# Local attention in 32-query blocks with a reordered chunk, in a program of two local-attention stacks

## What is computed

```python
x = x + attn_a(layernorm(x))
x = x + stack(layernorm(x))      # the diff touches both stacks
x = x + attn_b(layernorm(x))
x = x + stack(layernorm(x))
# stack: 6 times
x = attn_layer(shift_tokens(x)) + x
x = ffn_layer(shift_tokens(x)) + x
# attn_layer: q, k, v of 16 heads x 64; q and k to unit length, scaled, rotary tables;
# window w = 32: block i of 32 queries sees key blocks i - 1 and i (64 keys),
mask = (it < jb) | (it > jb + w) | (jb == -1)      # at most 33 of the 64
attn = softmax(where(mask, -max, q @ k.T * 8)); out = (attn @ v) @ Wo
```

## Time and profile before

| | |
|---|---|
| median of 3 runs | 5310.7 us |
| span of the profiled execution | 5297.4 us |
| PE busy | 4675.9 us, 88% |
| VectorE busy | 4003.6 us, 76% |
| ScalarE busy | 3636.0 us, 69% |
| GpSimd busy | 2657.4 us, 50% |
| queue q1 of DMAs | 331028 packets, 281.93 MB, 20.6% of 16 engines |

### The profile page before, as it was taken

One profiled execution on the slowest core, in us unless ns is written; L12 is line 12 of the kernel. 1 busy time (PEld: TensorE's weight loads), 2 busy tenths in 40 slices (PEclk: granted clock), 3 DMA queues, 4 the chain that ended last, 5 costly groups with the idle time before them and its releaser, 6 DMA issues. The chain is left out here.

```text
span 5297.4 us, 148317 instructions
## 1 busy us (share of the span) xinstructions
PE 4675.9 (88%) x45796; PEld 2897.7 (55%) x45796; DVE 4003.6 (76%) x8097; ACT 3636.0 (69%) x11780; POOL 2657.4 (50%) x2108
## 2 busy tenths in 40 slices
PE   5999999698898998989989767989989989899897
PEld 1333332366565665656656544665656656566565
DVE  7888886587786877868778546878868778687785
ACT  1777777586785876858768514867858778587684
POOL 3000000465665666656656404656656566566564
PEclk6999999899999999999999977999999999999998
DMA  0000000222222222222222302222222222222223
GB/s 13 1 2 1 2 1 1 85 59 72 59 59 77 59 71 60 59 77 59 64 66 60 83 7 85 59 73 59 57 78 59 72 62 57 77 60 69 65 56 93
DMA packets 332305, 288.20 MB, mean 54 GB/s; under 512 B 149102, under 2 KB 290964, under 8 KB 329748
## 3 DMA queue, kind: packets, MB, share of 16 engines
q1 hardware_dynamic: 331028, 281.93, 20.6%
q10 hardware_dynamic: 768, 0.02, 0.0%
HBM read 100.42 MB, written 30.41 MB: 25 GB/s over the span
## 5 line engine op out<-in xcount | busy, mean ns | idle before, releaser
L929 POOL TENSOR_TENSOR g_rn<-g_ss,g_minus_half 128x8 f32<-128x8 f32 x384 | 636.8, 1658 | 299.7 <-DVE g_ss L1077 297.0
L929 POOL TENSOR_TENSOR f_rn<-f_ss,f_minus_half 128x8 f32<-128x8 f32 x384 | 636.8, 1658 | 299.2 <-DVE f_ss L1077 295.9
L425 DVE TENSOR_REDUCE a_maxima<-a_max 128x1 f32<-128x512 f32 x1024 | 651.3, 685 | 148.4 <-PE a_max L539 142.2
L1003 ACT ACTIVATE f_ex<-f_bank,f_nmx 128x96 f32<-128x96 f32 x1536 | 501.5, 338 | 226.8 <-DVE f_nmx L1082 226.8
L1003 ACT ACTIVATE g_ex<-g_bank,g_nmx 128x96 f32<-128x96 f32 x1536 | 501.6, 338 | 226.6 <-DVE g_nmx L1082 226.6
L349 ACT ACTIVATE a_pex<-a_scores 128x512 f32<-128x512 f32 x1024 | 531.7, 607 | 159.6 <-PE a_scores L548 159.6
L934 POOL TENSOR_TENSOR f_qr<-f_t 128x512 f32<-128x512 f32 x384 | 488.4, 1272 | 268.8 <-DVE f_t L1100 268.8
L934 POOL TENSOR_TENSOR g_qr<-g_t 128x512 f32<-128x512 f32 x384 | 488.2, 1271 | 269.0 <-DVE g_t L1100 269.0
L1172 PE MATMUL g_bank<-g_wqkv,g_xT 128*128 128x512 f32 x768 | 407.2, 613 | 30.4 <-ACT g_xT L977 24.3
L1172 PE MATMUL f_bank<-f_wqkv,f_xT 128*128 128x512 f32 x768 | 406.4, 612 | 29.2 <-ACT f_xT L977 24.5
L1077 DVE TENSOR_REDUCE g_ss<-g_sq 128x8 f32<-128x512 f32 x384 | 263.1, 685 | 207.9 <-ACT g_sq L985 207.9
(11 more groups left out here) (244 smaller groups left out, 11909.8 us busy)
## 6 DMA issues: line engine op xcount, KB each, us to landing
f_vw<-f_vt SPq DMA_DIRECT2D x96, 384.0 KB, 4.3
g_vw<-g_vt SPq DMA_DIRECT2D x96, 384.0 KB, 4.3
f_vw<-f_vt SPq DMA_DIRECT2D x96, 256.0 KB, 3.5
g_vw<-g_vt SPq DMA_DIRECT2D x96, 256.0 KB, 3.5
f_vw<-f_vt SPq DMA_DIRECT2D x96, 128.0 KB, 2.3
g_vw<-g_vt SPq DMA_DIRECT2D x96, 128.0 KB, 2.3
f_wqkv<-in_f_Wqkv_dram SPq DMA_DIRECT2D x7, 1536.0 KB, 9.5
g_wqkv<-in_f_Wqkv_dram SPq DMA_DIRECT2D x7, 1536.0 KB, 9.3
```

The source lines that it names most:

```text
L425: dve.tensor_reduce(maxima[:, m // 4, m % 4:m % 4 + 1], ps_max[m % 3][:], AX.X, ALU.max).then_inc(dv_max, 1)
L929: pool.tensor_tensor(rn[:, b, :], ss[:, b, :], minus_half[:], ALU.pow).then_inc(pl_rn, 1)
L1003: last = act.activation(ex[:, b, u, :], ps_s[:, h, KEYS * jj:KEYS * jj + KEYS], ACT.Exp, bias=nmx[:, b, u:u + 1], accum_out=sm[:, b, u:u + 1])
```

## The change

- `BLK` goes from 64 to 32 (`NB` = 4 blocks per tile), so a block has 64 keys (`KEYS`) instead of 96.
- Scores: 16 products per chunk with 32 queries as weights and 64 keys moving, on eighths of the array (64x32). `kT` holds the keys of two tiles side by side, 128 columns each; an even tile's first block takes its previous keys from the other end of the buffer, in another order than the rest, and the mask has a form for it. The copy of the keys' tail and its semaphore go.
- Masks: 4 matmuls (64x64 parts) instead of 2.
- Probabilities: two tiles of 64 keys are turned together: 2 turnings of 128 columns instead of 4 of 96, and one copy of 128x256 instead of 96x512.
- Values: 16 products with 64 rows, on quarters of the array. `vw` holds 4 blocks, for two groups of heads in the two halves of the partitions: 10 DMAs per tile instead of 3. `vt`'s columns are ordered by pair for it. `ps_pT` and `ps_o` share a pair of banks, so the values wait for the copy of the probabilities turned in the same chunk.
- Output projection in halves, at c = 2 and c = 3; the values' projection at c = 0 and 1; the residual's addition at the end of c = 3 for tile t - 2 instead of t - 3 a chunk later.
- Order of the chunk on PE: projection, turning of q/k (n - 3 instead of n - 2), turning of probabilities, values' projection or half an output projection, values, masks and scores, x. On ScalarE: xT, exponentials (n - 5 instead of n - 4), q/k copy, copy of probabilities, squares, values' copy, output copy. On VectorE: rotary products (n - 2 instead of n - 1), normalisation, scaling, maxima, sum of squares, residual.

```diff
-BLK = 64
+BLK = 32
+NB = P // BLK
-        kT = sb("kT", [P, PAIRS, WINDOW + P])
+        kT = sb("kT", [P, PAIRS, 2 * P])
-        vw = sb("vw", [P, 2, 2, INNER])
+        vw = sb("vw", [P, 2, NB, PAIRS // 2 * P])
...
-                    sp.dma_start(vw[0:32, p, 0, :], vt[96:128, 1 - p, :]).then_inc(ld_vw[p], 16)
-                    sp.dma_start(vw[32:96, p, 0, :], vt[0:64, p, :]).then_inc(ld_vw[p], 16)
-                    sp.dma_start(vw[0:96, p, 1, :], vt[32:128, p, :]).then_inc(ld_vw[p], 16)
+                    for jj in range(2):
+                        k, cols = KEYS * jj, slice(512 * jj, 512 * jj + 512)
+                        last, mine = (k, k + WINDOW) if p else (k + BLK, k)
+                        sp.dma_start(vw[last:last + WINDOW, p, 0, :], vt[P - WINDOW:P, 1 - p, cols]).then_inc(ld_vw[p], 16)
+                        sp.dma_start(vw[mine:mine + BLK, p, 0, :], vt[0:BLK, p, cols]).then_inc(ld_vw[p], 16)
+                        for blk in range(1, NB):
+                            r = BLK * blk - WINDOW
+                            sp.dma_start(vw[k:k + KEYS, p, blk, :], vt[r:r + KEYS, p, cols]).then_inc(ld_vw[p], 16)
...
+                    if real(t, c, 3):
+                        pe.wait_ge(pl_qr, upto(pl_qr, L, n - 3))
+                        pe.wait_ge(act_qk, upto(act_qk, L, n - 4))
+                        for j in range(4):
+                            last = pe.transpose(ps_qkT[:, P * j:P * j + P], qr[:, 1 - b, P * j:P * j + P], ident[:])
+                        last.then_inc(pe_qkT, 1)
                     if real(t, c, 6):
...
                         pe.wait_ge(dv_pn, upto(dv_pn, L, n - 6))
+                        pe.wait_ge(act_aT, upto(act_aT, L, n - 8))
                         pe.wait_ge(act_pT, upto(act_pT, L, n - 7))
-                        for u in range(4):
-                            last = pe.transpose(ps_pT[0:KEYS, P * u:P * u + P], pn[:, b, u, :], ident[:])
+                        for h in range(2):
+                            last = pe.transpose(ps_pT[:, P * h:P * h + P],
+                                                pn[:, b, 2 * h:2 * h + 2, :].rearrange("p u c -> p (u c)"), ident[:])
                         last.then_inc(pe_pT, 1)
...
+                        for j in range(4 * half, 4 * half + 4):
+                            last = pe.matmul(ps_y[:, 0:P], aT[:, q, j, :], wo[:, j, :], start=(j == 0), stop=(j == PAIRS - 1))
...
+                        turned = min(n - 6, STEPS - 1) if known else n - 6
+                        pe.wait_ge(act_pT, upto(act_pT, L, turned)).then_inc(own["pe"], 1)
+                        for blk in range(NB):
+                            qs = slice(BLK * blk, BLK * blk + BLK)
+                            for jj in range(2):
+                                k = slice(KEYS * jj, KEYS * jj + KEYS)
+                                for h in range(2):
+                                    r = slice(DH * h, DH * h + DH)
+                                    at = P * g + DH * h
+                                    last = pe.matmul(ps_o[r, jj, qs], vw[k, p, blk, at:at + DH], pT[k, 1 - b, h, qs],
+                                                     start=True, stop=True, tile_position=(KEYS * jj, DH * h))
+                        last.then_inc(pe_o, 1)
...
+                        for jj in range(2):
+                            j = 2 * g + jj
+                            for blk in range(NB):
+                                o = slice(BLK * blk, BLK * blk + BLK)
+                                k0 = (0 if even else P) + BLK * blk - WINDOW
...
+                                    last = pe.matmul(ps_s[o, h, KEYS * jj:KEYS * jj + KEYS].rearrange("p (a k) -> p a k", k=WINDOW),
+                                                     qT[r, j, o], keys, start=False, stop=(jj == 1), tile_position=(DH * h, BLK * blk))
+                        last.then_inc(pe_s, 1)
```

More of the change, by code:

```diff
@@ L61, in host_tables @@
     seen = (c[None, :] >= q[:, None]) & (c[None, :] <= q[:, None] + WINDOW)
-    rest = np.where(seen, f(0), f(MASKED))
-    first = np.where(seen & (c[None, :] >= WINDOW), f(0), f(MASKED))
-    start = np.where(np.arange(P)[:, None] < BLK, first, rest)
-    mask = np.stack([np.stack([m, m], 1) for m in (start, rest)], 1)
+    odd = np.where(seen, f(0), f(MASKED))
+    before = np.arange(P)[:, None] % DH < BLK
+    even = np.where(before, np.roll(odd, -WINDOW, axis=1), odd)
+    first = np.where(before & (c[None, :] >= KEYS - WINDOW), f(MASKED), even)
+    mask = np.stack([np.stack([m, m], 1) for m in (first, even, odd)], 1)
     theta = (f(1.0) / np.power(f(10000.0), np.arange(0, AD, 2, dtype=f) / f(AD))).astype(f)
@@ L650, in bank @@
             return ctx.enter_context(nc.psum_tensor(f"{tag}_bank{i}", [P, n, 512], F32))
-        one = [bank(i) for i in range(6)]
+        one = [bank(i) for i in range(4)]
+        ps_po = bank(4, 2)
         ps_s = bank(6, 2)
-        banks = [t[:, 0, :] for t in one] + [ps_s[:, 0, :], ps_s[:, 1, :]]
+        banks = [t[:, 0, :] for t in one] + [ps_po[:, 0, :], ps_po[:, 1, :], ps_s[:, 0, :], ps_s[:, 1, :]]
         ps_qk = banks[0:2]
@@ L1147, in _ @@
                 dve.wait_ge(pl_rope, upto(pl_rope, L, 5)).then_inc(own["dve"], 1)
[L1148 removed]
+                layer(dve, tile, group, L, NT + 2)
                 dve.wait_ge(pe_s, upto(pe_s, L, STEPS - 1))
[L1151 removed]
+                dve.memset(kT[:, :, 2 * P - WINDOW:2 * P], 0.0).then_inc(dv_kzero, 1)
         @block.tensor
@@ new lines, in tile @@
+                        last.then_inc(pe_o, 1)
+                    if real(t, c, 4):
+                        g, even = c, q == 1
+                        first = known and t == 1
+                        if first and c == 0:
+                            pe.wait_ge(act_const, 3)
+                        pe.wait_ge(act_qk, upto(act_qk, L, 4 * t - (3 if g < 2 else 1)))
+                        pe.wait_ge(act_exp, upto(act_exp, L, n - 5)).then_inc(own["pe"], 1)
+                        for h in range(2):
+                            r = slice(DH * h, DH * h + DH)
+                            for o in (slice(0, DH), slice(DH, P)):
+                                seen = 2 if o.start or not even else 0 if first else 1
+                                pe.matmul(ps_s[o, h, 0:2 * KEYS], twice_bf[r, o], mask_bf[r, seen, :], start=True, stop=False,
+                                          tile_position=(DH * h, o.start))
@@ L1233, in tile @@
-                        last.then_inc(pe_o, 1)
-                    if c == 3 and real(t - 2, 0, 0):
-                        pe.wait_ge(act_aT, upto(act_aT, L, 4 * t - 5))
-                        pe.wait_ge(act_v, upto(act_v, L, min(2 * t, 2 * NT - 2) + 1 if known else 2 * t + 1))
-                        pe.wait_ge(dv_y, upto(dv_y, L, t - 3))
-                        for j in range(PAIRS):
-                            last = pe.matmul(ps_y[:, 0:P], aT[:, q, j, :], wo[:, j, :], start=(j == 0), stop=(j == PAIRS - 1))
-                        last.then_inc(pe_Wo, 1)
```

216 lines of the change are left out of this document (94 added, 122 removed).

## The result

The changed kernel takes 5255.1 us (median of 4 runs, 5248.4 to 5269.7), the kernel before 5307.6 beside it: ratio 0.991, 95% interval 0.989 to 0.992. It is faster, by 52 us where 336 were forecast, and outside the range of 4830 to 5240. The profiled execution spans 5251.2 (before 5297.4).

The account below looks back on a forecast made before the run. TensorE (PE) was taken as the bound: 14.73 us of work plus waits of 0.2, 0.2 and 0.1 made a tile of 15.25 instead of 17.27. At 28 us per layer, 336 for 12, 5310.7 became 4975 us (range 4830 to 5240).

Parts of the forecast that it names:

- the forecast sum 14.73: PE work per middle tile in us, added up group by group after the change; 1.65 less than before.
- rival (1): Small score and value products on PE don't run eight and four at once: tile 18.8, kernel 5555 us; chance 0.12 in full.
- Rival (2): PE's longer loop body no longer fits the instruction store: 3.5 us per branch, 168 in all, 5143 us; chance 0.12.
- Rival (4): Fewer waits than taken: 14.73 for all 15 intervals, 38.7 us less per layer, kernel 4847 us; chance 0.08.
- All stay below 14.73, so PE remains the bound: Middle tile: VectorE falls to 13.6 and ScalarE to 12.5, so PE's work still sets the tile.
- the new wait: Values on PE wait for the same chunk's copy of turned probabilities: 0 to 0.3 per chunk, taken as 0.05.
- 0.2 per tile, 0 to 1.1: ScalarE's copy of new values waits for the last of ten window DMAs; 0.2 us per tile taken.
- Rival (3): Value windows come late, plus the late copy of probabilities: tile 16.3 to 17, kernel 5080 to 5200 us; chance 0.12.
- Ramps at both ends gain less ... 1.7: Layer ends: 13 of 15 intervals gain in full, plus 1.7 us for the ramps, 28 us per layer.

Follow-up runs that it names:

- comb1: Changed kernel with scores issued ahead of values on TensorE, plus the edits of tail_first and exp_early: 5101.4 us, ratio 0.962 to the kernel before.
- pn_last: ss_first with VectorE's reciprocal and normalization moved behind the maxima: 5271.4 us, ratio 0.992 to the kernel before.
- both: pn_last with scores also issued ahead of values on TensorE; window DMAs as in the changed kernel: 5274.2 us, ratio 0.993 to the kernel before.
- tail_first: Changed kernel with the two window DMAs reading the previous tile's last rows issued first; ScalarE's copy waits for only these of the newest ten: 5174.6 us, ratio 0.975.
- comb2: both with the edits of tail_first and exp_early added: 5076.5 us, ratio 0.956 to the kernel before.
- half_vw: Changed kernel with five of each tile's ten window DMAs left out, so it computes something else: 5167.5 us, ratio 0.975 to the kernel before.
- exp_early: Changed kernel with the exponentials of a layer's last chunk issued at the end of tile 16, ahead of the feed-forward's first group: 5249.2 us, ratio 0.989.
- comb4: comb3 with fewer added identity transposes in tile 17 (3 per place, none ahead of the output projection): 5051.8 us, ratio 0.953 to the kernel before.
- ss_first: Changed kernel with VectorE's sum of squares issued ahead of the maxima in each chunk: 5514.0 us, ratio 1.039 to the kernel before.
- comb3: comb2 with unread identity transposes added on TensorE in each layer's drain: 5094.7 us, ratio 0.959 to the kernel before.

## Why the prediction was wrong, point by point

**TensorE's work: near, 0.1 to 0.3 low.** PE's busy time in a middle tile is 14.86 and 15.27, the forecast sum 14.73, and comb1's tile without idle time has 15.06 from start to start. In the timeline above, 32 values start 0.46 ahead of the masks, the masks 0.20 ahead of the scores, and the next projection starts 0.59 behind the scores (1131.86 to 1132.45). So rival (1) is out: the small products do run side by side, at 226 and 225 ns each but 32 within 0.67 and 0.46. Rival (2) is out too, by the branch of the tile loop (shortest/median/longest ns):

```profile
L762 PEldq COMPARE_BRANCH  x60: 76/212/242, 1071.7 to 5097.3; - x60
```

212 ns, not 3.5 us, for the longer body. VectorE at 13.87 (forecast 13.6) and ScalarE at 12.71 (12.5) are near. Rival (4)'s 38.7 us per layer can't be worked out from its words: 15 intervals of 14.73 against the 249.97 of before, 3 taken off for the ends, is 26, and added 32. Nothing else hangs on it.

**"All stay below 14.73, so PE remains the bound": the step that failed.** It compared sums of busy time and never followed a ring through the engines. The forecast even named the new wait ("they wait for the copy of this chunk ... since both halves lie in one bank ... the 36 instructions of mask and scores queue behind, and VectorE's maximum behind those"), and priced it by the cover ahead of it, at 0.05 per chunk. But the exponentials and the copies ahead of that copy on ScalarE start from the very maxima that queue behind. Its length could have been added up beforehand: scores, mask and values 1.1 and maxima 0.42 by the sum's own steps, the copy of probabilities 0.39, the copy of queries or keys 0.6 and four exponentials 1.3 by the trace of before, less 0.25 where ScalarE's work overlaps, and 0.3 for handing over: near 3.9, against 3.68 of PE work per chunk. (The last two terms were put in with the result known.) Four turns of the measured 3.88 are 15.5, 0.3 of the missing 0.6 of a tile; the other 0.3 is the fourth chunk's, where the maxima come 4.0 or 4.2 to 4.4 apart: no run takes that apart, and a longer fourth chunk is in comb2 too (4.1 to 4.5). The ring is a property of "values ahead of scores" and of one bank for both halves: with the scores first the wait fell from 90.6 to 14.4 (pn_last to both), and with the DMAs' wait gone too every second tile of the loop fell to 15.25 (tail_first to comb1).

**GpSimd was not priced at all.** Its rn grew from 1658 to 1897 ns since the new order puts the normalization onto the end of rn, and the second ring took the maxima in. Neither costs anything as long as the first ring is as long; pn_last shows that. Together with the scores first it matters: 25 us from comb1 to comb2.

**Window DMAs: right mechanism, wrong size.** "0.2 per tile, 0 to 1.1" would be 38 us for 192 tiles. Measured: nothing in the middle tiles, 0.4 to 1.6 in each of six tiles per layer at the ends (half_vw), 80 us in all (tail_first), and the middle tiles too once the rings are gone (both). What the sum lacked is that at the ends an issue is at times twice or three times 0.59; that these long issues make the wait is read from where they stand, no run takes them away. Rival (3), 5080 to 5200 by the DMAs and the late copy together, is the nearest to what happened, though 5255 is above it and the two causes hid each other instead of adding up.

**"Ramps at both ends gain less ... 1.7": wrong.** They gained less than nothing. Besides the DMAs, the drain grew: the result of a layer's last tile comes 32.0 behind that of the tile two before, where it was 26.2. Two causes have a measured size: the exponentials of chunk 63, issued a chunk later than before, fell behind the feed-forward's first copy (1.2 of the last interval, exp_early, though by itself that gave the kernel nothing clear of noise), and TensorE's clock fell to 1.2 GHz with the products at 1.08 instead of 0.67 and half an output projection at 2.07 instead of 1.06 (25 us in all at the least, comb2 to comb4; before, the same stretch ran at 1.00). The trace shows what TensorE did around the fall: it stood idle between the chunks of the drain, where the chain through the other engines sets the pace, 1.24 ahead of the values at 1252.16, 3.66 ahead of the feed-forward's transposes at 1270.09. The drain of the changed kernel also holds a normalization of 1.69 under GpSimd's product for the rotary tables, which wasn't tried by itself.

**What is left.** From 5255 to the 4975 of the forecast are 280 us. The runs account for 80 (DMAs' wait), 98 (rings, held normalization and exponentials, tail_first to comb2) and 25 (clock), to 5052. These shares go by the order of the edits: since the limits hide each other, another order would share them out otherwise. Of the last 77, some 24 are the loop's tiles (15.33 and 15.62 instead of 15.25, 9 by 0.22 by 12); most of the rest lies in the drain (the last two intervals take 27.6 where the forecast had some 24) and wasn't taken apart.

## What to carry to other kernels

When one engine is the fullest by busy time, add up every ring that an order by hand closes (each engine's queue order counts as an edge, and so does each wait for a shared bank) and compare the longest with the fullest engine's work per turn; a wait "covered" by work that itself depends on what queues behind the wait is not covered. When an experiment that removes a likely cause changes nothing, don't strike the cause: remove it together with its neighbours, since limits of a tuned kernel stand close together. And let a buffer's writer wait for those reads alone that touch what it overwrites: two DMAs of ten, here 80 us.

## What the runs showed of the hardware

**VectorE and GpSimd hold each other up.** A normalization that starts while GpSimd's addition runs (both read their inputs from SBUF) ends 0.28 behind the addition's end, at 1.44 instead of 0.42. In the changed kernel and comb1 one that starts 1.04 to 1.5 us into rn takes its 0.42, and rn 1.81 to 2.12 instead of 1.65; in pn_last, both and comb2 one that starts 0.2 to 1.0 into rn changes neither. With the normalization behind the maxima the means are 424 and 1660 ns (comb2). The Trainium skill, "SBUF — State Buffer", "Who interferes with whom", says that a VectorE instruction with two SBUF inputs contends with a GpSimd instruction that reads SBUF, that the lock on the shared ports is exclusive and whoever issues first has them for the whole instruction, and that tensor_reduce never contends. The held normalization agrees, and so do the reductions, 0.41 to 0.43 and 0.67 to 0.69 throughout. But the rotary products (two SBUF inputs as well) start 0.28 behind rn in ss_first (1129.75 against 1129.47), take their 0.68 and 0.68, and rn its 1.65: for this power of 8 elements per partition the lock did not last the whole instruction.

**TensorE's clock in a drain.** The granted clock was 1.00 up to 1250 in the changed kernel and 0.58 in the stretch of 15.67 in which PE had 9.0 of work with gaps of up to 3.66, 0.50 in comb2's; 55 added transposes of 128x128 per layer, many of them in gaps, kept it at 0.86 and gave back 25 us in all. Too many in the path (comb3) took more than the clock gave.

**A DMA's issue** on SyncE's queue took 0.54 to 0.61 for the windows of tiles 5 to 12 in every layer of the changed kernel, and up to 2.06 for those of tiles 2 to 4 and 13 to 15, in looped and in written-out code alike. The runs don't tell why.
